# Moments of the last normalisation moved from VectorE to ScalarE and GpSimd, exponentials stored with the head innermost

## The reference

```python
q = batchnorm(x @ w_q)                                  # 2 x 8 heads x 128
sim = einsum('pbnhd,hkpd->pbnhk', q, keys)              # 32 keys per half and head
sx, ix = top_k(sim[0], 8);  sy, iy = top_k(sim[1], 8)
scores, pk = top_k(sx[..., :, None] + sy[..., None, :], 8)
h = gelu(x . down_embed[indices]) * softmax(scores)
out = sum(h * up_embed[indices])
x = layernorm(x + out)                                  # no gain, no offset; this is the "last normalisation"
```

## Time and profile before

| | |
|---|---|
| median of 3 runs | 783.41 us (783.17 to 788.17) |
| profiled execution | 780.71 us |
| span of the profiled execution | 778.8 us |
| mean granted PE clock | 0.937 of full speed |
| busy over the span | PE 79%, DVE 78%, POOL 56%, ACT 45% |

### The profile page before, as it was taken

One profiled execution on the slowest core, in us unless ns is written; L12 is line 12 of the kernel. 1 busy time (PEld: TensorE's weight loads), 2 busy tenths in 40 slices (PEclk: granted clock), 3 DMA queues, 4 the chain that ended last, 5 costly groups with the idle time before them and its releaser, 6 DMA issues.

```text
span 778.8 us, 46654 instructions
## 1 busy us (share of the span) xinstructions
PE 618.8 (79%) x19783; PEld 513.8 (66%) x19783; DVE 609.4 (78%) x1879; ACT 346.9 (45%) x546; POOL 436.8 (56%) x680
## 2 busy tenths in 40 slices
PE   5888979999998977888547587677888777777784
PEld 4677868778877855556346476566777666676674
DVE  3566657776766757999855888899999999999982
ACT  3344534545444452655430444445554445455540
POOL 4222422333232323556521878878988888988881
PEclk9999999999999998999865689999999999999998
DMA  7511111111111110000000222322222222222221
GB/s 175 193 33 38 31 29 33 35 35 33 33 37 28 32 56 14 15 28 13 0 8 7 45 55 66 68 49 61 66 67 67 67 61 67 67 64 60 61 57 37
DMA packets 45362, 38.82 MB, mean 50 GB/s; under 512 B 6512, under 2 KB 40432, under 8 KB 45040
## 3 DMA queue, kind: packets, MB, share of 16 engines
q1 hardware_dynamic: 45296, 37.86, 19.4%
HBM read 16.86 MB, written 2.10 MB: 24 GB/s over the span
## 4 chain that ended last, share of the span: by engine, by line
PE 45%; DVE 36%; issue 15%; POOL 2%; ACT 1%; DVEq 1%; POOLq 0%; ACTq 0%
PE ps L651 12%; PE ps L664 8%; DVE top L1239 5%; PE ps L677 5%; PE ps L838 5%; DVE prod L1294 4%; PE ps L817 3%; DVE wq_sb L1270 3%; PE ps L646 3%; DVE r L1078 3%; DVE stats L1058 2%; DVE best L1250 2%; DVE r_x L1279 2%; DVE hidT L1285 2%; PE ps L826 2%
## 5 line engine op out<-in xcount | busy, mean ns | idle before, releaser
L1017 DVE TENSOR_REDUCE row_max<-ps 128x8 f32<-128x768 f32 x64 | 61.3, 958 | 77.4 <-PE ps L651 77.4
L838 PE MATMUL ps<-up_sb,prod 128*128 128x128 f32 x512 | 79.6, 317 | 48.0 <-DVE prod L1294 47.3
L465 POOL COPY v_ones<-v_raw 96x512 f32<-96x512 f32 x32 | 19.5, 609 | 169.4 <-DMA v_raw<-in_x_wrapped 160.1
L875 ACT ACTIVATE arena<-arena 128x768 f32<-128x768 f32 x64 | 54.0, 844 | 125.3 <-DVE arena L1020 125.3
L838 PEld LDWEIGHTS ps<-up_sb,prod 128*128 128x128 f32 x512 | 73.1, 224 | 54.6 <-DVE prod L1294 53.7
L651 PE MATMUL ps<-early 128*32 128x96 f32 x4096 | 103.3, 252 | 5.8 <-issue 5.7
L651 PEld LDWEIGHTS ps<-early 128*32 128x32 f32 x4096 | 87.8, 112 | 28.7 <-issue 28.7
L817 PE MATMUL ps<-arena,hidT 128*32 128x32 f32 x8192 | 81.7, 200 | 26.2 <-issue 21.2
L817 PEld LDWEIGHTS ps<-arena,hidT 128*32 128x32 f32 x8192 | 76.7, 112 | 31.6 <-issue 22.8
L568 POOL TENSOR_TENSOR wq_sb<-wq_sb,rel_exp 128x1024 f32<-128x1024 f32 x32 | 76.3, 2384 | 8.4 <-POOL rel_exp L564 7.0
L859 ACT ACTIVATE arena<-ps 96x512 f32<-96x512 f32 x128 | 68.6, 585 | 26.6 <-PE ps L664 26.5
(11 more groups left out here) (140 smaller groups left out, 1285.3 us busy)
## 6 DMA issues: line engine op xcount, KB each, us to landing
arena<-r_x SPq DMA_DIRECT2D x128, 128.0 KB, 2.4
v_raw<-in_x_wrapped SPq DMA_DIRECT2D x128, 48.0 KB, 1.8
arena<-in_x SPq DMA_DIRECT2D x8, 256.0 KB, 4.9
x_tile<-in_x SPq DMA_DIRECT2D x32, 64.0 KB, 1.7
x<-in_x SPq DMA_DIRECT2D x8, 256.0 KB, 2.8
xT_tile<-xT SPq DMA_DIRECT2D x32, 64.0 KB, 1.9
out<-out_tile SPq DMA_DIRECT2D x32, 64.0 KB, 1.6
wq_sb<-in_w_q SPq DMA_DIRECT2D x1, 1024.0 KB, 9.6
```

Of the source, the lines that this page charges most:

```text
L838: mm = nc.tensor.matmul(ps[:, 6 + p, 0:P], pairs[:, c // 2, c % 2], up_sb[:, c, :], start=False, stop=(c == EC - 1))
L1017: V.tensor_reduce(mx.rearrange("p (a b) -> p a b", a=2), sc, AX_X, ALU.max).then_inc(max_done, 1)
```

## The change

Three instructions of DVE (`last_moments`: BN_STATS, BN_AGGR, add of the constant) are gone. ACT gets two activations with a summing output: `last_sum(t-2)`, a copy of the 128 values that also gives their sum, is the first work of iteration t on ACT, and `last_square(t-2)`, the square of value less mean with its sum, stands between `rel_exps(t+1)` and `best_exps(t+1)`. POOL gets `last_mean(t-2)`, which makes minus the mean from the sum, and stands between `scale_right(t)` and `tops(t+1)`; and one more small instruction in `last_scale`, which makes the variance from the sum of squares. `last_square` waits for `last_mean`, and `last_mean` for `last_sum`.

The second part: `rel_exp` is laid out as 2 halves x 32 keys x 8 heads. ACT writes it with a step of 8 values; POOL's reads of it in `scale_right` and `scale_left` step from head to head by one value instead of 32.

```diff
-        rel_exp = two("rel_exp", [P, PH, KEYS])
+        rel_exp = two("rel_exp", [P, 2, KEYS, PK_HEADS])
...
-                ey = rel_exp[p][:, PK_HEADS:PH, :]
-                nc.gpsimd.tensor_tensor(ey, ey, bcast(rz[p][:], 2, KEYS), ALU.mult).then_inc(scaled, 1)
+                ey = rel_exp[p][:, 1]
+                nc.gpsimd.tensor_tensor(ey, ey, bcast(rz[p][:], 1, KEYS), ALU.mult).then_inc(scaled, 1)
...
-                nc.gpsimd.tensor_tensor(right[p], right[p], bcast(ey.rearrange("p h j -> p j h"), 3, TERMS), ALU.mult
+                nc.gpsimd.tensor_tensor(right[p], right[p], bcast(ey, 3, TERMS), ALU.mult
                                         ).then_inc(right_ready, 1)
...
-                ex = rel_exp[p][:, 0:PK_HEADS, :].rearrange("p h i -> p i h")
+                ex = rel_exp[p][:, 0]
...
+            def last_mean(t):
+
+                pool.wait_ge(d_sum, t + 1)
+                hold(pool)
+                nc.gpsimd.tensor_scalar(minus_mean4[:], sum4[:], -1.0 / P, 1.0, ALU.mult, ALU.mult).then_inc(d_mean, 1)
+
             def last_scale(t):
 
-                pool.wait_ge(d_var, t + 1)
+                pool.wait_ge(d_square, t + 1)
+                hold(pool)
+                nc.gpsimd.tensor_scalar(var4[:], square4[:], 1.0 / P, EPS, ALU.mult, ALU.add).then_inc(rstd_step, 1)
+                pool.wait_ge(rstd_step, 2 * t + 1)
                 hold(pool)
                 nc.gpsimd.tensor_tensor(rstd4[:], var4[:], minus_half[:, 0:1], ALU.pow).then_inc(rstd_step, 1)
-                pool.wait_ge(rstd_step, t + 1)
-                hold(pool)
-                nc.gpsimd.tensor_scalar(shift4[:], mom4[:, 0:1], rstd4[:], -1.0, ALU.mult, ALU.mult).then_inc(d_rstd, 1)
+                pool.wait_ge(rstd_step, 2 * t + 2)
+                hold(pool)
+                nc.gpsimd.tensor_tensor(shift4[:], minus_mean4[:], rstd4[:], ALU.mult).then_inc(d_rstd, 1)
 
             def d_pool(i):
                 for p in range(2):
                     t, o = 2 * i + p, 1 - p
                     if have(t):
                         scale_right(t, p)
+                    if have(t - 2):
+                        last_mean(t - 2)
                     if have(t + 1):
                         tops(t + 1, o)
...
-                nc.scalar.activation(rel_exp[p][:].rearrange("p a k -> p (a k)"), ps[:, p, :], ACT.Exp
+                nc.scalar.activation(rel_exp[p][:].rearrange("p a k h -> p a h k"),
+                                     ps[:, p, :].rearrange("p (a h k) -> p a h k", a=2, h=PK_HEADS), ACT.Exp
                                      ).then_inc(relexp_done, 1)
+
+            def last_sum(t, p):
+                a.wait_ge(up_done, t + 1)
+                nc.scalar.activation(scratch[:], ps[:, 6 + p, 0:P], ACT.Copy, accum_out=sum4[:]).then_inc(d_sum, 1)
+
+            def last_square(t, p):
+                a.wait_ge(d_mean, t + 1)
+                nc.scalar.activation(scratch[:], ps[:, 6 + p, 0:P], ACT.Square, bias=minus_mean4[:], accum_out=square4[:]
+                                     ).then_inc(d_square, 1)
...
             def d_act(i):
                 for p in range(2):
                     t, o = 2 * i + p, 1 - p
+                    if have(t - 2):
+                        last_sum(t - 2, p)
                     if have(t + 1):
                         rel_exps(t + 1, o)
+                    if have(t - 2):
+                        last_square(t - 2, p)
+                    if have(t + 1):
                         best_exps(t + 1, o)
                     if have(t - 2):
                         last_norm(t - 2, p, i - 1)
...
-            def last_moments(t, p):
-                v.wait_ge(up_done, t + 1)
-                V.bn_stats(stats4[:], ps[:, 6 + p, 0:P]).then_inc(d_step, 1)
-                v.wait_ge(d_step, 2 * t + 1)
-                need(v, out_ready, t)
-                hold(v)
-                V.bn_aggr(mom4[:], stats4[:]).then_inc(d_step, 1)
-                v.wait_ge(d_step, 2 * t + 2)
-                V.tensor_scalar(var4[:], mom4[:, 1:2], EPS, None, ALU.add).then_inc(d_var, 1)
```

More of the change, by code:

```diff
@@ L193, in attention_and_product_keys @@
         out_tile = two("out_tile", [P, P])
-        stats4 = sb("stats4", [P, 6])
-        mom4 = sb("mom4", [P, 2])
+        scratch = sb("scratch", [P, P])
+        sum4 = sb("sum4", [P, 1])
+        minus_mean4 = sb("minus_mean4", [P, 1])
+        square4 = sb("square4", [P, 1])
         var4 = sb("var4", [P, 1])
@@ L289, in attention_and_product_keys @@
         up_done = sem("up_done")
-        d_step = sem("d_step")
-        d_var = sem("d_var")
+        d_sum = sem("d_sum")
+        d_mean = sem("d_mean")
+        d_square = sem("d_square")
         rstd_step = sem("rstd_step")
@@ L1216, in _ @@
             v.wait_ge(c_row_done, 2)
-            c_rest = rel_exp[0][:].rearrange("p a k -> p (a k)")
+            c_rest = rel_exp[0][:].rearrange("p a k h -> p (a k h)")
             V.tensor_copy(c_rows[:], ps[:, 7, :]).then_inc(c_step, 1)
@@ L1313, in d_dve @@
                         top_keys(t + 1, o)
-                    if have(t - 2):
-                        last_moments(t - 2, p)
                     if have(t):
```

## The result

The changed kernel takes 876.15 us (median of 4 runs, 875.44 to 877.74), against 783.29 us for the kernel before in its 4 runs: a ratio of 1.1178, with a 95% interval of 1.1125 to 1.1231. It is 93 us slower. The forecast was 830 us with a range of 815 to 850: the direction is right, the size is half of what came.

The account below looks back on a forecast made before the run. DVE was taken to set the tile's period, POOL close behind. First tile 3.7, written-out start 4.5, loop 33.7, written-out end 4.5 and last tile 0.9 gave +47.3 us: 828.0 profiled, 830 forecast, range 815 to 850.

Parts of the forecast that it names:

- The bound of before: Last stage: a tile's period of about 10 us is DVE's work, with POOL close behind.
- The new wait and its place: POOL before `last_mean`, ahead of `tops`: waits some 2 us per tile for `last_sum`, queued behind ACT's gelus and table loads.
- that ring: Last stage, ACT and POOL: `last_norm` through tables, `last_sum`, `last_mean`, `tops` to next `last_norm`; 11.76 us per tile against 10.36.
- rival (b): Last stage: the ACT and POOL ring with PE slower at a lower granted clock; 31 us more, 861 us; chance 0.06.
- "some 0.3 us" of slack: PE's way from `up_projection` to half of `down`: of 1.4 us growth at a lower clock, some 0.3 us are slack.
- the other ring: The ring over ACT and POOL in the last stage, forecast at 11.76 us per tile.
- Rival (a): Last stage: the ACT and POOL ring, with the `rel_exp` layout worth nothing on POOL; 15 us more, 845; chance 0.12.
- Rival (c): Last stage: no ring if the sum is ready by 612.84; period falls by DVE's 0.7 us, 761 us; chance 0.03.
- The written-out iterations: Last stage, two periods before and two after the loop: +4.5 us at each end.
- the first tile: Start of the last stage: the first `tops` behind a `last_mean` comes at 456.91 instead of 453.24, +3.7 us.
- The last chain: Last tile, nothing covers its chain: the new moments take some 2.0 us, less 1.1 that went, +0.9 us.
- The factor reads: POOL's products without 128-byte steps between heads: -0.53 us for `scale_left`, -0.50 us for `scale_right`.

Follow-up runs that it names:

- experiments 2 and 3: The changed kernel with, in 2, `last_mean` behind `tops` on POOL: 805.14 us; in 3, `last_sum` one iteration earlier on ACT: 790.73 us.
- experiment 4: The changed kernel with 16 extra, unused 128 x 128 matmuls per iteration in PE's wait ahead of `up_projection`: 846.17 us, ratio 1.0738.
- experiment 6: The changed kernel with 8 extra, unused matmuls per iteration in PE's wait, in the looped iterations alone: 861.64 us, ratio 1.0963.
- experiment 5: The changed kernel with the old layout of `rel_exp` and 16 extra, unused matmuls per iteration in PE's wait: 860.33 us, ratio 1.0881.
- experiment 1: The changed kernel with the old layout of `rel_exp` (head before key), the moments as changed: 877.53 us, ratio 1.1132.

## Why the prediction was right and where it was wrong

- **The bound of before** was read rightly. DVE set the period: the layout alone took 6.4 of 100 us from POOL and nothing from the time.
- **The new wait and its place** were right. POOL waits in front of `last_mean` for a sum that stands behind two table loads in ACT's queue, and all of POOL's iteration waits behind it. Two moves of one instruction each (experiments 2 and 3) take away 71 and 85 of 93 us. The wait was forecast at some 2 us; it is 3.6 in the changed kernel and 2.07 with the clock held up (experiment 4).
- **The length of that ring**, 11.76 us, measured 11.87 where it alone decides. Of its terms: ACT 4.28 forecast and 4.32 measured (644.03 to 648.35); `last_sum` with hand-over 0.66 and 0.63; `last_mean` 0.21 and 0.19; `tops` to the next `last_norm` 6.61 (6.75 - 0.53 + 0.39) and 6.73. `scale_left` fell to 1.60 us and not to 1.47.
- **The step that failed** is the sentence that the ring closes "over ACT and POOL", together with rival (b), to which I gave 0.06 and 31 us. In the forecast the slower PE is a term of nothing. I took PE's part to be off the ring with "some 0.3 us" of slack and its clock as a mishap that the earlier trace rows at 0.97 spoke against. In fact the new wait empties PE too: its wait ahead of `up_projection` grows from some 2 us to 3.5 and 3.9, and with it the clock falls in every looped tile, where before it fell in 3 of 22, just on the way that has next to no slack. PE's way grew by 1.64 us (6.65 less 5.01) in the tile shown and by 2.35 in its neighbour; without that its ring would be 13.34 - 1.64 = 11.70 us, only 0.17 below the other ring. The period grew from 11.87 to 13.58. 24 looped tiles times 1.71 us are 41 us of the 44 by which the loop was off (77.4 against 33.7); the other 3 are the 0.11 by which the ring itself was short. Experiment 4 gave back 36.7 us in the loop (325.98 less 289.26), with its first three tiles still slow. Experiment 4 shows that the clock is the cause: the order of every queue stays, PE has more to do, the clock is full and the period is that of the other ring. Experiment 6 shows the same tile by tile. What exactly makes the clock fall around such a wait stays open: the wait's length alone doesn't decide it (experiment 6).
- **Rival (b) was also mis-sized.** I scaled 4 us by 2.92/2.15 from one slow L838. What ran at half speed was `similarities` and the second half of `up_projection`, in every other tile all of it, with `down` pushed behind them whole: the limit was the second half of `down`, not the first.
- **Rival (a)** had its mechanism right at full clock (0.41 us a tile, experiment 5) and wrong in the kernel as it is (0, experiment 1).
- **Rival (c)** and its condition: with the sum in time, the ring is gone, as it said. The 761 us that I wrote for it are not: two more POOL instructions with a gap make POOL full, and the period stays near 10 us at best (9.84 and 10.41 with the clock held up). POOL saves 0.8 us in its two products and gets 0.6 us back in the new instructions, the gap and the slower small product.
- **The written-out iterations** were short by 1.4 and 3.0 us and the first tile by 0.7. `up_projection` takes 3.6 to 3.8 us in four of them as well; that this is the whole reason is not shown. The last chain was 1.3 us too dear.
- **The factor reads**: by the rows I expected 1.47 and 1.89 us, measured are 1.60 and 2.00. The line that I read them against runs through L542 itself, so it could not show that a repeated factor costs nothing. By the page of the Trainium skill, "GPSIMD Engine Reference", section "Performance pitfalls for Q7 kernels", the steps above 8 bytes would have been worth an estimated 0.64 us in `scale_left`; 0.40 came. The direction holds, both sizes were too large.

## What to carry to other kernels

Before moving work to an engine with idle time, look at where in its queue the idle time lies, and at what stands ahead of the place that the work is given: with a 0.3 us instruction behind two table loads and two gelus the change cost 93 us, and with it in another place of the same queue 5. When a new wait makes a ring, walk every engine that hangs on it, not the two that are waited for; the one with little slack is priced again with what the longer wait does to its clock. Where an engine's clock is at stake, look at the granted clock by pieces of one tile, not at the mean of a stretch: 0.80 on average was 1.00, 0.75, 0.50 and 0.96.

## What the runs showed of the hardware

- A summing activation is two instructions in the profile: the activation (0.28 us for 128 x 128 from PSUM) and an ACTIVATION_READ_ACCUMULATOR of 0.19 us that starts 0.18 us after the first did; the next activation starts 0.27 us after the first. With a bias operand 0.34 and 0.21 us.
- Writing the exponentials with a step of 8 values (32 bytes) took 1.09 to 1.12 us on average instead of 0.60 for the same 128 x 512.
- On POOL, neighbouring factors instead of ones 128 bytes apart took the products from 2.39 to 2.00 us and from 2.00 to 1.60 us; the small product in place (256 values, its second factor now stepping rather than repeated in runs) went from 0.62 to 0.73 us.
- A matmul of fp32 values, 128 x 128, is two rows of the profile, and 0.24 us at the full clock (16 of them are 32 rows and 3.84 us in experiment 4).
- PE's granted clock fell around each of the two waits shown (3.45 and 3.91 us), in one of them not in the wait but in the work behind it. In the kernel before, with waits of 1.6 to 2.2 us, it fell in 3 of 22 tiles; in experiment 6, with 1.8 to 2.4 us, in 13 of 21. With the wait filled to 0.6 us or less (experiment 4) it stayed full.
- `outer` pauses for some 2 us in the written-out tiles and in the first body of the loop, and not in the later ones, with nothing in the trace that it waits for, in the kernel before and in every other run.
